# Keys of the second attention: two-part operands and three single-pass products in place of one fp32 product

## The chip, the cores and the metric

The kernel runs on one core of one Trainium2 chip. The metric is the time of one execution on the device in microseconds (us); for the kernel before, the median of three runs is shown. A core has five engines with instruction queues of their own: TensorE (PE in the profile; PEld are its weight loads), VectorE (DVE), ScalarE (ACT), GpSimd (POOL) and SyncE (SP, which only issues DMAs here). They meet through semaphores: an instruction can wait until a counter reaches a value, and can raise one when it is done.

## The reference

The program is two transformer layers on 16 sequences of 128 tokens with 128 features; `ctx_1024` are 16 contexts of 120 rows. Each layer is a cross-attention to the context and a feed-forward part with 8 experts of which 2 are used per token.

```python
x = x + L0_xattn(layernorm(x), ctx, ctx, ...)   # 16 heads of 8 features, a temperature per head from a small MLP
x = x + L0_ffn(layernorm(x), ...)               # top 2 of 8 experts, hidden size 256
x = x + L1_xattn(layernorm(x), ctx, ctx, ...)   # 8 heads of 128 features, windows of 64 positions, dilations 1, 2, 4, 8
x = x + L1_ffn(layernorm(x), ...)               # top 2 of 8 experts, hidden size 64
```

In `L1_xattn` the queries and keys of head h are `x Wq[h]` and `ctx Wk[h]` with biases, and their dot products are the scores. The kernel folds both weights into one matrix per head, so that "keys" of a head are the context times a 128x128 matrix, and the queries are the normalized x itself.

## The kernel before

One program text per engine, written by hand; nothing schedules it, and the order on an engine is the order of the text. A helper, `software_pipeline`, takes stages with lags and writes them out step by step, one sequence after the other (`peel=NB`: no hardware loop). The program has five parts: (a) statistics of the first attention's scores (to about 114 us); (b) the first attention and the routing, with POOL scattering rows to a table in memory sorted by expert (to about 192 us); (c) the first experts, 39 tiles of 128 rows, which PE, ACT and DVE work on while SP loads and stores tiles (to about 257 us); (d) the second attention, sequence by sequence; (e) the second experts, the first of them mixed into the last steps of (d).

The change touches (d). Its operands: `ctxS` holds the 16 contexts, turned and with their rows in an order by dilation, 128 columns each; `qk1` holds the folded matrices of the 8 heads, written by ACT (line 660) at the start of (b); `vo1` the same for values and output. The function `d_keys(p, half)` on PE (lines 1774 to 1783) makes the keys of a pair p of sequences for four heads: four products of a 128x128 matrix with 256 columns of `ctxS`, each into half a PSUM bank, in full fp32. ACT (line 802), and in the first two pairs DVE too (line 1429), adds `uvec` and writes them to `keys`. There are 8 pairs with 2 halves. Four halves (`EARLY_PAIRS = 2`) stand ahead of the pipeline of (d), behind PE's last expert tile; the other twelve are one per step, from the third step on.

A step of (d) on PE: turn the attention weights and the norms (line 1545), keys (1781), output of whole heads (1838), values (1794), scores (1814, 1820), more values (1800, 1804), more output (1843). DVE has in a step: the scores with the window (1436, 1439, 1442), the residual (1461), the two expert rows of a later sequence gathered from memory and added (1413, 1417), norms (1150, 1160, 1178), and the attention weights (1447, 1449, 1453). ACT has the evictions of values (767) and turned weights (794), of norms (710, 697), the exponentials (773, 776) and the keys (802). POOL gathers rows by indirect DMA (983, two per sequence) and does the reciprocal roots (914, 916) and small sums.

Ahead of its gathers POOL has a stretch of its own: the low part `w1_lo` of the second experts' first weights (958), `b2h`, `b2l` and `b2t` (962 to 971) out of their biases. Rounded types (`F32R`, fp32r in the profile) are used in the kernel before already in (e): line 1857 makes a product as high times high, high times low and low times high, and line 1890 multiplies the gates with `b2t`.

Buffers are shared by hand: `shared(name, ...)` lays several tiles over one place, and `area(at, n)` cuts columns from `work`. Here `w1_hi` and `w1_lo` lie over `kT`, the keys of the first attention.

Of the kernel before, what the change touches and what calls it, by code (L numbers as in the profile page):

```python
# [8 lines left out]
F32 = mybir.dt.float32  # L9
F32R = mybir.dt.float32r  # L10
BF16 = mybir.dt.bfloat16
U32 = mybir.dt.uint32
ALU = mybir.AluOpType
# [3 lines left out]
P = 128  # L17


NB, LQ, LK, D = 16, 128, 120, 128  # L20
H0, DK0 = 16, 8
DH0 = 64
NE = 8
HID0 = 256
H1, E1 = 8, 128
# [3 lines left out]
F1 = 64  # L29
# [12 lines left out]
SEQS = 4  # L42
# [167 lines left out]
def build(nc, cols, widths, t, out):  # L210
    with ExitStack() as ctx:
        def sb(name, shape, dt=F32):
            return ctx.enter_context(nc.sbuf_tensor(name, shape, dt))[:]

        def shared(name, shape, parts):

            with nc.sbuf_tensor(name, shape, F32) as a:
                whole = a[:]
            return whole, [sb(*part) for part in parts]

        def sem(name):
            return ctx.enter_context(nc.semaphore(name))

        psum = ctx.enter_context(nc.psum_tensor("psum", [P, 8, 512], F32))
        BANK_KEEP, BANK_TAIL = 7, 6


        first, smalls, late = (sb(name, [P, widths[name]]) for name in ("first", "small", "late"))

        def of_pack(name):  # L230
            for pack, whole in (("first", first), ("small", smalls), ("late", late)):
                if name in cols[pack]:
                    return whole[:, cols[pack][name]]
# [4 lines left out]
        ctxS = sb("ctxS", [P, NB, P])  # L238

        qT, (b2t,) = shared("qT", [P, NB, LQ], [("b2t", [P, 2, 2, SEQS, D], F32R)])  # L240
        kT, (w1_hi, w1_lo, _) = shared("kT", [P, NB, LK], [
            ("w1_hi", [P, NE * F1], F32R), ("w1_lo", [P, NE * F1], F32R), ("kT_rest", [P, NB * LK - 2 * NE * F1], F32)])
        v0 = sb("v0", [LK, NB, D])

        xT, (x_hi,) = shared("xT", [P, NB, LQ], [("x_hi", [P, NB, LQ], F32R)])

# [9 lines left out]
        small = sb("scratch", [P, 8, BH])  # L256
# [6 lines left out]
        routerT, w2T, w3c = of_pack("router0"), of_pack("w2")[0:DH0], of_pack("w3")[0:DH0]  # L263
        w1f = sb("w1f", [P, 3, DH0])
        w1b = of_pack("w1").rearrange("p (c h) -> p c h", c=3)
        qk1 = sb("qk1", [P, H1, D])
        vo1 = sb("vo1", [P, H1, D])
        uvec = sb("uvec", [P, H1])
        router1, rb1, b2rows, b1e = (of_pack(n) for n in ("router1", "rb1", "b2rows", "b1e"))
# [17 lines left out]

        work, (gm, _) = shared("work", [P, 13552], [  # L290
            ("gm", [P, 2, SEQS, LQ], F32R), ("work_rest", [P, 13552 - 2 * SEQS * LQ], F32)])

        def area(at, n):
            return work[:, at:at + n]
# [5 lines left out]
        wcT = area(W_C, 1024).rearrange("p (h o) -> p h o", h=H1)  # L300

        wa, (_, b2h, gT, split, _, c_area, _, rows_r, _) = shared("wa", [P, 8688], [
            ("wa_h1", [P, 2560], F32), ("b2h", [P, D], F32R), ("gT", [P, 2, P], F32R),
            ("split", [P, 2, 2, 2, SEQS * NE], F32R), ("wa_b2l", [P, D], F32), ("c_area", [P, 4096], F32), ("wa_rows", [P, H1_TILES * P], F32),
# [73 lines left out]
        def banks(a, n, parts=P):  # L378
# [4 lines left out]
        rank_ps = keep[:, 512 - SLOTS * NE:512]  # L383
        total_ps = keep[0:1, 192:192 + NE]

        in_c = (area(13184, 12).rearrange("p (z s) -> p z s", z=2), area(13196, 4).rearrange("p (z s) -> p z s", z=2),
                area(13200, 8).rearrange("p (z s) -> p z s", z=2),
                c_area[:, 3840:4096].rearrange("p (z d) -> p z d", z=2), None)

        names = ("bn6", "mv", "rstd", "xn", "xnT")  # L390
# [39 lines left out]
        wt_ps, wt_act = sem("wt_ps"), sem("wt_act")  # L430
# [25 lines left out]
            sem("d_" + n) for n in ("kps", "keys_dve", "keys_act", "s", "sm", "max", "exp", "rs", "a", "tp", "aT", "vwp", "vw", "y", "x"))  # L456
        l1_folded, kept = sem("l1_folded"), sem("kept")
        b_xb, d_xb = sem("b_xb"), sem("d_xb")
        rounded, halved = sem("rounded"), sem("halved")
        e_gt, e_gts, e_h, e_g, e_gm, e_gps, e_hg, e_y, e_acc = (  # L460
            sem("e_" + n) for n in ("gt", "gts", "h", "g", "gm", "gps", "hg", "y", "acc"))
        e_split, e_out = sem("e_split"), [sem("e_out0"), sem("e_out1")]
# [88 lines left out]
        PRODUCTS = 4  # L551
# [38 lines left out]
        def keys_bank(p, half):  # L590
            return 2 * half if p < EARLY_PAIRS else 0
# [235 lines left out]
        def _(pool):  # L827
# [140 lines left out]
            for n in range(4):  # L968
                at, i = divmod(n, 2)
                of, rows = ((b2h[:, :].bitcast(F32), own[:, at, :]), (b2l, by_group[:, at, 0, :]))[i]  # L970
                nc.gpsimd.tensor_tensor(b2t[:, at, i], of.unsqueeze(1).to_broadcast([P, SEQS, D]),
                                        rows.unsqueeze(2).to_broadcast([P, SEQS, D]), ALU.mult).then_inc(halved, 1)

            def gather(b):
                r = b % RING_C
                if b == 0:
                    for s in range(RING_C):
                        pool.wait_ge(st_ct[s], 16 * len(range(s, TILES, RING_C)))
                if b >= RING_C:
                    pool.wait_ge(c_added, b - RING_C + 1)  # L980
                for j in range(2):
                    i = slot_of(j, b)
                    nc.gpsimd.indirect_dma_start(y_rows[:, r, j, :], None, by_expert[:, :],  # L983
                                                 bass.IndirectOffsetOnAxis(rows_at[:, i:i + 1], 0)).then_inc(ld_y[r], 16)
# [558 lines left out]
        def _(pe):  # L1543
            def turn(dst, src, k):
                return nc.tensor.transpose(dst, src, ident[0:k, 0:k])  # L1545
# [97 lines left out]
            for half in range(2):  # L1643
                m = turn(psum[:, 5, half * P:(half + 1) * P], small[:, 2, half * P:(half + 1) * P], P)
# [129 lines left out]
            def d_keys(p, half):  # L1774
                evicted = 2 * p + half if p >= EARLY_PAIRS else 2 * p + half - 1
                if evicted > 0:
                    pe.wait_ge(d_keys_dve, min(evicted, 2 * EARLY_PAIRS))
                    pe.wait_ge(d_keys_act, evicted)
                bank = keys_bank(p, half)
                for i in range(4):  # L1780
                    m = nc.tensor.matmul(psum[:, bank + i // 2, 2 * P * (i % 2):2 * P * (i % 2 + 1)], qk1[:, 4 * half + i, :],  # L1781
                                         ctxS[:, 2 * p:2 * p + 2, :].rearrange("p b s -> p (b s)"), start=True, stop=True)
                m.then_inc(d_kps, 1)

            def d_next_keys(b, z):
                if EARLY_PAIRS <= b // 2 + 1 < NB // 2:
                    d_keys(b // 2 + 1, b % 2)
# [131 lines left out]

            pe.wait_ge(halved, 1)  # L1920
            pe.wait_ge(ld_late, 32)
            for half in range(2 * EARLY_PAIRS):
                d_keys(*divmod(half, 2))
            c_turn = tail_turn("c")
# [46 lines left out]
```

## Time and profile before

| | us |
|---|---|
| median of 3 runs | 415.02 (414.48 to 415.03) |
| the profiled execution's own time | 413.28 |
| its span, first to last instruction | 411.5 |
| PE busy in the span | 353.8 (86%) |
| DVE busy | 303.3 (74%) |
| ACT busy | 271.8 (66%) |
| POOL busy | 196.9 (48%) |
| L1781, the keys, PE busy | 29.8 |

Busy times of engines overlap, so their shares say nothing of what sets the end; that is read from the chain that ended last, which is followed back from the last instruction to what released it at each step, and from the idle times of the engines. The mean duration of a matmul contains its way through the array (380 ns for L1781), and matmuls are pipelined: what one costs in a row of them is the distance between starts. An fp32 product shows as two instructions, a rounded one as one. PEclk is the clock granted to TensorE as a share of 2.4 GHz.

### The profile page before, as it was taken

What the parts mean: (1) busy time and instruction counts of PE and PEld (TensorE: products, weight loads), DVE (VectorE), ACT (ScalarE), POOL (GpSimd) and SP (SyncE); (2) the same over time, 40 slices, a digit from 0 to 9 for tenths busy, and PEclk for the clock granted to TensorE, in tenths of its full rate; (3) what the DMA queues carried; (4) which work ended last, traced back from release to release, by engine and by line L of the source; (5) the groups of instructions that cost most, each with busy time, mean ns of one, the idle gap of its engine ahead of it and who ended that gap; (6) DMA issues with size and microseconds to landing.
All of it is one profiled execution on the core that took longest, in us unless ns stands there. A gap on an engine that the chain in (4) does not pass through costs nothing.

```text
span 411.5 us, 11910 instructions
## 1 busy us (share of the span) xinstructions
PE 353.8 (86%) x4049; PEld 269.5 (65%) x4049; DVE 303.3 (74%) x1127; ACT 271.8 (66%) x813; POOL 196.9 (48%) x295
## 2 busy tenths in 40 slices
PE   2988897682599999973999999888999999968997
PEld 0524362341276767752999998757888888756886
DVE  5399989988428999996764444378898888885852
ACT  2499998986265657542578886457878778672440
POOL 4785878811002215667783000478878783532200
PEclk9988789986589999995799999989999999996999
DMA  7975739700000000112343332111001010000011
GB/s 234 338 212 160 223 100 335 322 1 0 3 2 6 6 5 18 37 34 70 105 116 92 97 92 57 37 33 41 27 23 28 17 28 2 2 2 2 4 49 51
DMA packets 36202, 30.97 MB, mean 75 GB/s; under 512 B 3504, under 2 KB 33584, under 8 KB 35504
## 3 DMA queue, kind: packets, MB, share of 16 engines
q1 hardware_dynamic: 33520, 24.98, 19.2%
q0 software_dynamic: 2048, 4.20, 3.5%
q10 hardware_dynamic: 576, 1.05, 0.7%
q8 instruction: 33, 0.54, 0.6%
q14 instruction: 25, 0.20, 0.2%
HBM read 14.94 MB, written 15.14 MB: 73 GB/s over the span
## 4 chain that ended last, share of the span: by engine, by line
PE 56%; DVE 19%; ACT 9%; issue 8%; POOL 4%; DMA 4%; POOLq 0%; DVEq 0%; SPq 0%; ACTq 0%
PE psum L1753 9%; ACT wa L649 6%; PE psum L1705 5%; PE psum L1545 4%; PE psum L1781 4%; PE psum L1764 4%; DVE scored L1089 3%; DVE scored L1076 3%; PE psum L1585 3%; PE psum L1894 3%; PE psum L1804 2%; PE psum L1688 2%; PE psum L1857 2%; DVE work L1131 2%; PE psum L1820 2%
## 5 line engine op out<-in xcount | busy, mean ns | idle before, releaser
L649 ACT ACTIVATE wa<-psum,scored 128x120 f32<-128x120 f32 x256 | 69.5, 436 | 3.8 <-DVE scored L1076 3.8
L983 POOL DMA_INDIRECT c_area<-by_expert,rows_at x32 | 31.4, 980 | 51.3 <-DMA by_expert<-c_area 39.7
L1089 DVE BATCH_NORM_STATS2 scored<-wa 128x6 f32<-128x240 f32 x128 | 43.1, 398 | 1.6 <-issue 0.8
L1076 DVE TENSOR_REDUCE scored<-psum 128x8 f32<-128x960 f32 x32 | 36.5, 1142 | 9.9 <-PE psum L1585 9.9
L682 ACT ACTIVATE work<-psum 120x1024 f32<-120x1024 f32 x32 | 31.0, 1021 | 18.8 <-PE psum L1693 18.8
L1753 PE MATMUL psum<-c_area,work 128*128 128x128 f32 x312 | 43.3, 284 | 0.0
L1585 PE MATMUL psum<-wa,qT 64*128 64x480 f32 x128 | 41.0, 725 | 2.3 <-ACT wa L649 2.3
L1753 PEld LDWEIGHTS psum<-c_area,work 128*128 128x128 f32 x312 | 39.7, 200 | 0.1
L910 POOL TENSOR_TENSOR rstd<-rstd,eps 128x2 f32<-128x2 f32 x16 | 12.5, 784 | 55.0 <-DVE rstd L1165 55.0
L866 POOL TENSOR_TENSOR wa<-kT,first 128x960 f32<-128x960 f32 x16 | 28.6, 1791 | 16.6 <-PE psum L1585 16.6
L942 POOL DMA_INDIRECT by_expert<-scored,rows_at x32 | 32.2, 1006 | 8.9 <-issue 8.3
L1335 DVE TENSOR_TENSOR c_area<-psum,c_area 128x256 f32<-128x256 f32 x39 | 16.5, 424 | 26.4 <-ACT c_area L748 22.9
L1781 PE MATMUL psum<-ctxS,qk 128*128 128x256 f32 x128 | 29.8, 380 | 0.0
L773 ACT ACTIVATE work<-work,d 128x128 f32<-128x128 f32 (+1 forms) x64 | 23.1, 370 | 5.8 <-DVE d L1439 5.8
L743 ACT COPY work<-upT 128x512 f32 x39 | 24.2, 621 | 2.4 <-issue 2.4
L767 ACT COPY work<-psum 128x1024 f32<-128x1024 f32 x16 | 16.2, 1011 | 14.0 <-PE psum L1804 13.9
L1781 PEld LDWEIGHTS psum<-ctxS,qk 128*128 128x128 f32 x128 | 23.7, 193 | 2.6
L1764 PE MATMUL psum<-dnT,c_area 128*128 x156 | 24.4, 280 | 0.6 <-DVE c_area L1335 0.6
L802 ACT ACTIVATE work<-psum,uvec 128x256 f32<-128x256 f32 x56 | 22.0, 471 | 2.7 <-PE psum L1781 2.7
L782 ACT ACTIVATE wa<-psum,late 128x512 f32<-128x512 f32 x16 | 10.8, 685 | 19.2 <-DVE c_area L1476 10.8
L1131 DVE RECIPROCAL work<-psum 128x128 f32<-128x128 f32 x16 | 15.3, 954 | 10.0 <-PE psum L1705 9.5
L748 ACT ACTIVATE c_area<-psum 128x256 f32<-128x256 f32 x39 | 14.9, 383 | 11.1 <-PE psum L1753 11.1
(264 smaller groups left out, 945.0 us busy)
## 6 DMA issues: line engine op xcount, KB each, us to landing
by_expert<-work SPq DMA_DIRECT2D x12, 768.0 KB, 7.6
c_area<-by_expert SPq DMA_DIRECT2D x39, 64.0 KB, 1.8
by_expert<-c_area SPq DMA_DIRECT2D x39, 64.0 KB, 1.6
upT<-in_up_dram SPq DMA_DIRECT2D x1, 2048.0 KB, 13.7
work<-in_heads_dram SPq DMA_DIRECT2D x1, 1536.0 KB, 8.9
late<-in_late_dram SPq DMA_DIRECT2D x1, 1098.0 KB, 10.3
x<-in_x_dram ACTq DMA_DIRECT2D x4, 256.0 KB, 5.6
ctxS<-in_ctx_classes_dram SPq DMA_DIRECT2D x1, 1024.0 KB, 10.0
```

Of the source, the lines that this page charges most:

```text
L649: e = nc.scalar.activation(prob[:, z, head, :], psum[:, score_bank(b, half) + h // 4, (h % 4) * LK:(h % 4 + 1) * LK], ACT.Exp, bias=rowneg ...
L682: nc.scalar.activation(probT[:, z, half * HALF0:(half + 1) * HALF0, :].rearrange("p h q -> p (h q)"), psum[0:LK, 2 * half:2 * half + 2, :] ...
L743: nc.scalar.copy(ct_w[:, n % 2, :], upT[:, bass.ds(e * UP_TILES, UP_TILES), :].rearrange("p t c -> p (t c)")).then_inc(ct_we, 1)
L866: nc.gpsimd.tensor_tensor(kexp[:, z], kT[:, b, :].unsqueeze(1).to_broadcast([P, HALF0, LK]), halfscale.unsqueeze(2).to_broadcast([P, HALF0 ...
L942: nc.gpsimd.indirect_dma_start(by_expert[:, :], bass.IndirectOffsetOnAxis(rows_at[:, i:i + 1], 0), xrow[:, BATCH * r + i % BATCH, :], None ...
L983: nc.gpsimd.indirect_dma_start(y_rows[:, r, j, :], None, by_expert[:, :], bass.IndirectOffsetOnAxis(rows_at[:, i:i + 1], 0)).then_inc(ld_y ...
L1076: nc.vector.tensor_reduce(rowneg[:, b * H0:(b + 1) * H0].rearrange("p (a c h) -> p a c h", a=2, c=2)[:, :, half], banks(score_bank(b, half ...
L1089: s = nc.vector.bn_stats(bnout[:, bass.ds(b * HALF0 + h // 2, 1), :].rearrange("p a s -> p (a s)"), prob[:, z, h:h + 2, :].rearrange("p h ...
L1585: m = nc.tensor.matmul(psum[:, score_bank(b, half) + g, 0:4 * LK], qT[rows, b, :], kexp[rows, z, 4 * half:4 * half + 4].rearrange("p i k - ...
L1753: m = nc.tensor.matmul(psum[:, n % 2, j * P:(j + 1) * P], ct_w[:, n % 2, j * P:(j + 1) * P], ct_xT[:, n % 2, :], start=True, stop=True)
L1764: m = nc.tensor.matmul(psum[:, 4, 0:D], ct_h[:, n % 2, j * P:(j + 1) * P], w, start=(j == 0), stop=(j == DN_TILES - 1))
L1781: m = nc.tensor.matmul(psum[:, bank + i // 2, 2 * P * (i % 2):2 * P * (i % 2 + 1)], qk1[:, 4 * half + i, :], ctxS[:, 2 * p:2 * p + 2, :].r ...
```

## The change

Every key product becomes three products of rounded operands (fp32r) that are summed in PSUM: high part of the matrix times high part of the context, high times low, and low times high. The high part is the operand rounded by a cast, the low part is the operand less its high part, rounded. POOL makes the four arrays once, between the biases `b2t` and the first gather: `qk_lo` (first used for the rounded copy), `ctx_hi`, then `qk_lo` itself, `qk_hi` over `qk1`'s own place, and `ctx_lo`. PE waits for the fifth of these ahead of its first keys.

Places: `w1_lo` moves over the first attention's weights in `first`; `qk_lo` lies over `kT`, `ctx_hi` over `v0`, `ctx_lo` over columns 11264 to 13312 of `work`, and the small tiles of the c norms move from column 13184 to 13448.

```diff
-        kT, (w1_hi, w1_lo, _) = shared("kT", [P, NB, LK], [
+        kT, (w1_hi, qk_lo, _) = shared("kT", [P, NB, LK], [
...
-        qk1 = sb("qk1", [P, H1, D])
+        qk1, (qk_hi,) = shared("qk1", [P, H1, D], [("qk_hi", [P, H1, D], F32R)])
...
+            pool.wait_ge(wt_act, PRODUCTS)
+            nc.gpsimd.tensor_copy(qk_lo[:, :, :], qk1[:, :, :]).then_inc(split_keys, 1)
+            nc.gpsimd.tensor_copy(ctx_hi[:, :, :], ctxS[:, :, :]).then_inc(split_keys, 1)
+            pool.wait_ge(split_keys, 1)
+            nc.gpsimd.tensor_tensor(qk_lo[:, :, :], qk1[:, :, :], qk_lo[:, :, :].bitcast(F32), ALU.subtract).then_inc(split_keys, 1)
+            pool.wait_ge(split_keys, 3)
+            nc.gpsimd.tensor_copy(qk_hi[:, :, :], qk1[:, :, :]).then_inc(split_keys, 1)
+            nc.gpsimd.tensor_tensor(ctx_lo[:, :, :], ctxS[:, :, :], ctx_hi[:, :, :].bitcast(F32), ALU.subtract
+                                    ).then_inc(split_keys, 1)
...
                 for i in range(4):
-                    m = nc.tensor.matmul(psum[:, bank + i // 2, 2 * P * (i % 2):2 * P * (i % 2 + 1)], qk1[:, 4 * half + i, :],
-                                         ctxS[:, 2 * p:2 * p + 2, :].rearrange("p b s -> p (b s)"), start=True, stop=True)
+                    for j, (left, right) in enumerate(((qk_hi, ctx_hi), (qk_hi, ctx_lo), (qk_lo, ctx_hi))):
+                        m = nc.tensor.matmul(psum[:, bank + i // 2, 2 * P * (i % 2):2 * P * (i % 2 + 1)], left[:, 4 * half + i, :],
+                                             right[:, 2 * p:2 * p + 2, :].rearrange("p b s -> p (b s)"), start=(j == 0), stop=(j == 2))
                 m.then_inc(d_kps, 1)
...
             pe.wait_ge(halved, 1)
             pe.wait_ge(ld_late, 32)
+            pe.wait_ge(split_keys, 5)
             for half in range(2 * EARLY_PAIRS):
                 d_keys(*divmod(half, 2))
```

On PE, a step of (d) with a half of the keys (row L1781), before (names: `psum<-` and the two operands, then the output's size and how many follow each other; an fp32 product is one row entry here):

```order
L1545 MATMUL psum<-first,c_area 128x128
L1781 MATMUL psum<-ctxS,qk 128x256 x4
L1838 MATMUL psum<-work 128x128 x2
L1794 MATMUL psum<-vo,ctxS 128x256
L1814 MATMUL psum<-work,xT 128x256
L1820 MATMUL psum<-work,xT 32x128 x8
```

The same place now; lines have moved by 13 to 16, and the three rows of L1797 are the last of the four heads' triples:

```order
L1797 MATMUL psum<-ctx_hi,qk_hi 128x256
L1797 MATMUL psum<-ctx_lo,qk_hi 128x256
L1797 MATMUL psum<-ctx_hi,qk_lo 128x256
L1854 MATMUL psum<-work 128x128 x2
L1810 MATMUL psum<-vo,ctxS 128x256
L1830 MATMUL psum<-work,xT 128x256
L1836 MATMUL psum<-work,xT 32x128 x8
```

Four products have become twelve; nothing else of the step has moved on PE. On POOL, the end of its own stretch and the first gather, before (in brackets the semaphores waited for):

```order
L971 TENSOR_TENSOR b2t<-b2h,own 128x512 [waits halved,b_qexp]
L971 TENSOR_TENSOR b2t<-wa,first 128x512
L971 TENSOR_TENSOR b2t<-b2h,own 128x512
L971 TENSOR_TENSOR b2t<-wa,first 128x512
L983 DMA c_area<-by_expert,rows_at 128x128 [waits st_ct2,st_ct3,st_ct1,st_ct0]
```

And now:

```order
L976 TENSOR_TENSOR b2t<-wa,first 128x512
L980 CAST qk_lo<-qk 128x1024 [waits wt_act]
L981 CAST ctx_hi<-ctxS 128x2048
L983 TENSOR_TENSOR qk_lo<-qk,qk_lo 128x1024 [waits split_keys]
L985 CAST qk_hi<-qk 128x1024 [waits split_keys]
L986 TENSOR_TENSOR ctx_lo<-ctxS,ctx_hi 128x2048
L998 DMA c_area<-by_expert,rows_at 128x128 [waits st_ct2,st_ct3,st_ct1,st_ct0]
```

Five instructions have come in between the biases and the gather. DVE, ACT and SP have the same instructions in the same order as before.

## Rows read from the trace of the kernel before

**Rows 1.** The page's costliest groups; the key products (busy us, mean ns, idle before).

```profile
L1781 PE MATMUL psum<-ctxS,qk 128*128 128x256 f32 x128 | 29.8, 380 | 0.0
```

**Rows 2.** Windows: length, busy us of PE, PEld, DVE, ACT, POOL, PEclk, DMA share, GB/s.

```profile
266.00:268.00 2.00, 0.22 (x1) 0.14 (x1) 1.56 (x6) 0.00 (x0) 1.29 (x3) 1.00 0.00 0
268.00:272.00 4.00, 3.45 (x29) 1.64 (x32) 2.04 (x9) 1.36 (x2) 3.20 (x5) 0.62 0.13 33
...
280.00:346.00 66.00, 64.77 (x1104) 56.68 (x1092) 57.08 (x248) 53.45 (x175) 51.07 (x95) 1.00 0.09 24
...
366.00:372.00 6.00, 2.47 (x28) 1.83 (x28) 5.57 (x24) 5.53 (x17) 1.44 (x4) 0.94 0.00 0
372.00:378.00 6.00, 5.44 (x28) 4.19 (x29) 2.61 (x10) 0.69 (x1) 1.43 (x4) 0.50 0.01 3
```

**Rows 3.** The chain that ended last (start us, us, engine, tile, line), second attention.

```profile
261.31 3.73 DMA c_area<-by_expert,rows_at
...
283.00 0.77 PE psum L1545 x5
283.77 1.73 PE psum L1781 x8
...
340.70 1.73 PE psum L1781 x8
...
346.67 0.68 DVE work L1436
```

**Rows 4.** PE in order of time, second experts.

```profile
385.01 0.39 PE L1857 MATMUL psum<-x_hi,w_lo 128*128 128x512 f32 x1
385.25 0.40 PE L1890 MATMUL psum<-b2t,gT 128*128 128x256 f32 x2
385.48 1.95 PE L1894 MATMUL psum<-late,c_area 128*128 128x128 f32 x16
387.18 0.48 PE L1890 MATMUL psum<-b2t,gT 128*128 128x256 f32 x2
387.50 1.95 PE L1894 MATMUL psum<-late,c_area 128*128 128x128 f32 x16
```

**Rows 5.** One step in order of time, all engines (start us, us, engine, instruction).

```profile
301.26 1.01 ACT L767 COPY work<-psum 128x1024 f32<-128x1024 f32 x1 [1.17 <-PE psum L1804]
...
305.02 0.28 DVE L1447 TENSOR_REDUCE d<-work 128x4 f32<-128x128 f32 x1 [0.48 <-ACT work L776]
...
305.57 0.99 DVE L1453 TENSOR_TENSOR work<-work,d 128x256 f32<-128x256 f32 x3
...
307.91 0.33 PE L1545 MATMUL psum<-first,work 128*128 128x128 f32 x1
```

**Rows 6.** DVE in order of time, first steps of the second attention.

```profile
282.86 0.68 DVE L1436 TENSOR_TENSOR work<-psum,late 128x512 f32<-128x512 f32 x1
...
289.04 0.68 DVE L1436 TENSOR_TENSOR work<-psum,late 128x512 f32<-128x512 f32 x1
...
293.54 1.09 DVE L1453 TENSOR_TENSOR work<-work,d 128x256 f32<-128x256 f32 x3
...
294.81 0.68 DVE L1436 TENSOR_TENSOR work<-psum,late 128x512 f32<-128x512 f32 x1
...
300.51 0.68 DVE L1436 TENSOR_TENSOR work<-psum,late 128x512 f32<-128x512 f32 x1
```

**Rows 7.** PE in order of time, first steps of the second attention.

```profile
295.22 0.66 PE L1545 MATMUL psum<-first,work 128*128 128x128 f32 x4
```

**Rows 8.** Groups of POOL by form (busy us, mean ns).

```profile
L927 POOL TENSOR_TENSOR x_lo<-xnT,x_hi 128x128 fp32r<-128x128 f32 x16 | 7.6, 472 | 1.3
...
L925 POOL CAST x_hi<-xnT 128x128 fp32r<-128x128 f32 x16 | 4.5, 283 | 1.8 <-ACT xnT L710 1.8
```

**Rows 9.** POOL in order of time, ahead of the gathers.

```profile
219.16 1.04 POOL L971 TENSOR_TENSOR b2t<-wa,first 128x512 fp32r<-128x512 f32 x1
259.91 1.09 POOL L983 DMA_INDIRECT c_area<-by_expert,rows_at  x1 [39.70 <-DMA by_expert<-c_area]
```

More of the change, by code:

```diff
@@ L225, in build @@
         BANK_KEEP, BANK_TAIL = 7, 6
-        first, smalls, late = (sb(name, [P, widths[name]]) for name in ("first", "small", "late"))
+        first, (w1_lo, _) = shared("first", [P, widths["first"]], [
+            ("w1_lo", [P, NE * F1], F32R), ("first_rest", [P, widths["first"] - NE * F1], F32)])
+        smalls, late = (sb(name, [P, widths[name]]) for name in ("small", "late"))
         def of_pack(name):
@@ L240, in build @@
         qT, (b2t,) = shared("qT", [P, NB, LQ], [("b2t", [P, 2, 2, SEQS, D], F32R)])
-        kT, (w1_hi, w1_lo, _) = shared("kT", [P, NB, LK], [
-            ("w1_hi", [P, NE * F1], F32R), ("w1_lo", [P, NE * F1], F32R), ("kT_rest", [P, NB * LK - 2 * NE * F1], F32)])
-        v0 = sb("v0", [LK, NB, D])
+        kT, (w1_hi, qk_lo, _) = shared("kT", [P, NB, LK], [
+            ("w1_hi", [P, NE * F1], F32R), ("qk_lo", [P, H1, D], F32R), ("kT_rest", [P, NB * LK - NE * F1 - H1 * D], F32)])
+        v0_rows, (ctx_hi,) = shared("v0", [P, NB, D], [("ctx_hi", [P, NB, P], F32R)])
+        v0 = v0_rows[0:LK]
         xT, (x_hi,) = shared("xT", [P, NB, LQ], [("x_hi", [P, NB, LQ], F32R)])
@@ L286, in build @@
         xnT = sb("xnT", [P, 2, LQ])
-        work, (gm, _) = shared("work", [P, 13552], [
-            ("gm", [P, 2, SEQS, LQ], F32R), ("work_rest", [P, 13552 - 2 * SEQS * LQ], F32)])
+        W_LOW = 11264
+        work, (gm, _, ctx_lo, _) = shared("work", [P, 13552], [
+            ("gm", [P, 2, SEQS, LQ], F32R), ("work_mid", [P, W_LOW - 2 * SEQS * LQ], F32), ("ctx_lo", [P, NB, P], F32R),
+            ("work_rest", [P, 13552 - W_LOW - NB * P], F32)])
         def area(at, n):
@@ L384, in build @@
         total_ps = keep[0:1, 192:192 + NE]
-        in_c = (area(13184, 12).rearrange("p (z s) -> p z s", z=2), area(13196, 4).rearrange("p (z s) -> p z s", z=2),
-                area(13200, 8).rearrange("p (z s) -> p z s", z=2),
+        in_c = (area(13448, 12).rearrange("p (z s) -> p z s", z=2), area(13460, 4).rearrange("p (z s) -> p z s", z=2),
+                area(13464, 8).rearrange("p (z s) -> p z s", z=2),
                 c_area[:, 3840:4096].rearrange("p (z d) -> p z d", z=2), None)
@@ L458, in build @@
         b_xb, d_xb = sem("b_xb"), sem("d_xb")
-        rounded, halved = sem("rounded"), sem("halved")
+        rounded, halved, split_keys = sem("rounded"), sem("halved"), sem("split_keys")
         e_gt, e_gts, e_h, e_g, e_gm, e_gps, e_hg, e_y, e_acc = (
```

## The prediction

> **What bounds the kernel now.** I read the page's costliest groups first, then the windows with the clock, the chain that ended last, one step of the second attention engine by engine, and last the rows that hold the new form of instruction. The group of L1781 is what the change edits: 128 instructions for 64 fp32 products, so two instructions a product, 29.8 us of TensorE (PE) busy time [rows 1]. Where they stand decides what they are worth. From 280 to 346 us PE is busy 64.77 of 66 us at the full clock, 2.4 GHz, and every other engine has room [rows 2]; the chain runs there through PE alone, and one half of the keys, 1.73 us, comes round in each step from 283.77 to 340.70 us: ten halves at nine intervals, (340.70 − 283.77)/9 = 6.33 us a step [rows 3]. In that stretch the step is PE's own sum, and what PE loses in work the step loses.
>
> Outside it the halves are not on the path. The first four stand before 264 us, while the chain goes through the gather's DMA (261.31, 3.73 us); PE is busy only 0.22 us from 266 to 268 [rows 2, 3]. The half before 283 us is followed by a wait of PE for VectorE (DVE), since the chain comes from POOL and DVE there and enters PE only at 283.00 [rows 3]. The twelfth half of the loop stands after 346.67 us, where the chain has passed to DVE's scores and the expert choice [rows 3]. So 10 halves of 16 count.
>
> **What a half costs before and after.** Before: 4 products, 8 instructions, 1.73 us, or 0.216 an instruction with two passes over 256 columns. After: 4 × 3 = 12 instructions of one pass over the same 256 columns, rounded operands (fp32r), each with a weight load of 128 columns as now. The trace holds that form: the two 128x256 fp32r products of L1890 start at 385.25 and the next line at 385.48, 0.115 each; the 512-column one ahead takes 385.25 − 385.01 = 0.24, about the double [rows 4]. So a half becomes 12 × 0.115 = 1.38 us, and a step loses 0.35. Ends: at the tempo of a pass of the old instructions, 0.216/2 = 0.108, a half is 1.30 and the step loses 0.43; in the other L1890 pair, whose two products take 387.50 − 387.18 = 0.32 [rows 4], one costs 0.16, a half 1.92, and the step grows by 0.19. I take 0.115, since the products of a half stand in a row without a wait, as at 385.25, where the pair at 387.18 follows a wait and other work. Break-even is 1.73/12 = 0.144.
>
> Beside the row of 0.115, the Trainium skill ("FP8 and Floating Point Precision", TensorE Precision Notes) has an fp32 product as four passes, high and low parts each with each; by that three passes of four would be 1.30 us, and the sum 10 × 0.43. The row of L1890 lies nearer and decides.
>
> **Who is late next.** In a step of the stretch VectorE waits 0.48 us for ScalarE's (ACT's) exponentials (305.02), and ACT waits 1.17 us for PE (301.26): both follow PE and come earlier with it. The last of DVE's products that PE turns ends at 305.57 + 0.99 = 306.56, PE reaches the turn at 307.91 [rows 5]: 1.35 us to spare, of which 0.35 go. Without that wait DVE fills 6.33 − 0.48 = 5.85 us of a step, so at 5.98 it still fits. ACT's evictions of the keys (after the exponentials) keep their place. One place gives something back: early in the stretch DVE is behind. Its product of 293.54 ends at 294.63, and PE turns it at 295.22 [rows 6, 7]. Two shortened halves ahead would bring PE there at 295.22 − 0.70 = 294.52, so PE waits some 0.15 to 0.2 us, once, as DVE's next round (294.81 to 300.51, 5.70 us [rows 6]) is shorter than PE's 5.98. I subtract 0.2.
>
> **What is added.** GpSimd (POOL) gets five instructions ahead of the gathers: casts of 1024, 2048 and 1024 columns, differences of 1024 and 2048. No row has these sizes. From below: nothing less than zero. From above, by the 128-column rows times 8 and 16, with the fixed part of each counted as often: casts 0.283 × 32 = 9.1, differences 0.472 × 24 = 11.3, together 20.4 us [rows 8]. They start behind POOL's last product, 219.16 + 1.04 = 220.2, and POOL does nothing until the gather at 259.91, a wait of 39.70 us for the expert stage's stores [rows 9]. Ending at 240.6 at the latest, they are done before PE's first keys at about 257, whose new wait stands behind the last expert tile: cost 0. Queued behind that wait are the keys, values and turns, nothing else; behind the casts on POOL the gathers and the normalizations, which wait anyway. Without the cover a microsecond past 259.9 would cost a microsecond. The casts' own wait is for copies of the first attention's stage, long past. The new places of the buffers (the low part of the expert weights, the small tiles at 13448) move no instruction; on ACT, DVE and SP the order stays as it was.
>
> **The sum.** 10 × 0.35 − 0.2 = 3.3 us. The profiled execution takes 413.28 us, span 411.5 and 1.8 around it; 413.28 − 3.3 = 409.98. The median of the runs shown is 415.02, 1.74 above that execution; added again, 411.7 us. The likeliest case's own range is 410.4 to 413.4: 0.43 or about 0.2 saved a step (411.0 or 413.2), and some 0.6 below or 0.2 above for the spread of the runs shown.
>
> **Rivals.** *Clock.* The granted clock is 0.62 from 268 to 272 us and 0.50 (1.2 GHz) from 372 to 378, each time after PE had been idle for much of the time (busy 0.22 of 2 us and 2.47 of 6 just ahead); the later stretch has 5.44 us of PE work [rows 2]. The change makes PE idle 1.4 us earlier ahead of 268 (four halves, 0.35 each) and moves the later stretch against the clock's falls. If the second fall is missed, half of 5.44, 2.7 us, is won: 409.0. If one falls as long on work now at full clock, 2.7 are lost: 414.4. For it: both falls stand at PE's idle places, which move. Against: the idle places remain, with the same length at the later one. The first is worth less: 3.45 us at 0.62 would be 2.1 at the full clock, 1.3 us [rows 2]. Chance 7% each way.
>
> *DVE takes over.* If DVE's rounds cannot follow, with its waits for ACT and POOL, and stay near the 6.18 us of one early round (scores at 282.86 and 289.04), a step loses only 0.15: 1.5 us, 413.5. For it: that round, and how little of a step DVE has free. Against: its rounds of 5.77 and 5.70 us right after [rows 6], and ACT's part, which PE releases. Chance 14%.
>
> *Weight loads stand outside: slower.* In a half 12 loads follow each other instead of 8, behind shorter products. If a load isn't drawn ahead, the pair at 387.18 [rows 4] gives the price: 0.16 a product, 1.92 a half, 0.19 × 10 = 1.9 us more, 416.9. It decides from 0.144 a product on. Against: the pair at 385.25 has two loads and takes 0.115 each. Chance 8%.
>
> On this the Trainium skill ("TensorE: Matmul & The Clock Gate", Part 3, The mechanism) says that a weight load overlaps a running product only where the row groups differ, and here all 128 rows are used. By that rule each of the loads would stand beside its product and the kernel would be slower, as in this rival. The trace speaks against it, with 0.115 for a load and a product of 256 columns.
>
> That the rounded operands would not bring single passes I leave out: 0.115 for 256 columns excludes it.
>
> **How the numbers follow.** Forecast 64%, clock 14%, DVE 14%, loads 8%. What a measurement of this kernel can tell from no change is 0.2%, 0.83 us, so faster means under 414.2. Faster: 62 of the 64, 7 of the clock, 12 of DVE's 14: 81%. Slower, over 415.85: the 8 of the loads and 1 of the others: 9%. The same: 10%. The range reaches on the low side to the won clock and on the high side past DVE's case and the lost clock: 409.0 to 414.6.
>
> **What would show it.** In the profile of the changed kernel: 12 of PE's instructions in a half, where there are 8, and 1.38 us for it on the chain, steps of 5.98 us between 280 and 343 us, DVE's wait for ACT at about 0.13; POOL's splits between 220 and 241 and the first gather still at about 260 behind the store's DMA and no wait of PE's for the splits. Wrong it would be if a half takes 1.7 us or more, if steps stay at 6.2 or above with PE waiting for DVE, if the gather moves, or if PE works at 1.2 GHz in another stretch than 268 to 272 and 370 to 376.

## The result, and the profile after

The changed kernel takes 411.5 us (median, 410.25 to 413.72) and the kernel before 415.02 (413.4 to 417.01) on the same chip: ratio 0.9923, 95% interval 0.9899 to 0.9946, so 2.2 to 4.2 us faster. The forecast was 411.7. On another chip, with two altered kernels beside it, the same changed kernel took 410.51 against 415.78 (0.9883, 0.984 to 0.9927).

The profiled execution takes 411.19 us, its span is 409.4 (before 411.5). The answers to [rows 1] are the key products of the page before, now three groups by operands (columns: count, then shortest, median and longest in ns, first and last start):

```profile
L1797 PE MATMUL psum<-ctx_hi,qk_hi x64: 279/280/365, 258.6 to 345.8; 128*128 128x256 f32 x64
L1797 PE MATMUL psum<-ctx_lo,qk_hi x64: 278/281/290, 258.8 to 345.9; 128*128 128x256 f32 x64
L1797 PE MATMUL psum<-ctx_hi,qk_lo x64: 277/281/285, 258.9 to 346.1; 128*128 128x256 f32 x64
```

192 instructions where there were 128, but what one costs in a row of them is the distance of starts. PE in order of time, a half of the changed kernel and what follows it:

```profile
302.45 0.36 PE L1797 MATMUL psum<-ctx_hi,qk_hi 128*128 128x256 f32 x1
302.65 0.28 PE L1797 MATMUL psum<-ctx_lo,qk_hi 128*128 128x256 f32 x1
302.76 0.28 PE L1797 MATMUL psum<-ctx_hi,qk_lo 128*128 128x256 f32 x1
302.88 0.28 PE L1797 MATMUL psum<-ctx_hi,qk_hi 128*128 128x256 f32 x1
...
303.82 0.28 PE L1797 MATMUL psum<-ctx_hi,qk_lo 128*128 128x256 f32 x1
303.95 0.61 PE L1854 MATMUL psum<-work 128*128 128x128 f32 x4
```

From 302.65 to 303.82 ten products pass, 0.117 to 0.118 each. The windows that answer to [rows 2], shifted by the gain (length, busy us of PE, PEld, DVE, ACT and POOL, PEclk, DMA share, GB/s):

```profile
268.00:272.00 4.00, 2.78 (x21) 1.42 (x21) 2.29 (x9) 1.36 (x2) 3.22 (x6) 0.80 0.12 33
...
280.00:343.00 63.00, 61.69 (x1128) 55.56 (x1132) 56.40 (x241) 53.77 (x177) 50.87 (x95) 1.00 0.10 26
363.00:369.00 6.00, 3.06 (x37) 2.42 (x35) 5.54 (x26) 5.65 (x16) 1.44 (x4) 1.00 0.00 0
369.00:375.00 6.00, 4.81 (x30) 3.65 (x29) 2.80 (x9) 1.06 (x3) 1.43 (x4) 0.53 0.00 0
```

PE is still busy almost throughout from 280 to 343 us (61.69 of 63), at 2.4 GHz; the stretch at about 1.2 GHz behind PE's idle place is there as before. The chain that ended last, against [rows 3]:

```profile
262.98 2.94 DMA c_area<-by_expert,rows_at
...
283.47 0.95 POOL c_area L998
...
287.33 0.95 POOL c_area L998
...
290.32 0.82 DVE d L1454 x3
...
291.80 0.68 PE psum L1854 x4
...
296.66 1.42 PE psum L1797 x12
...
302.69 1.42 PE psum L1797 x12
```

A half is 1.42 us where it was 1.73. But the chain runs through POOL's gathers and DVE until 291.80 us; before, PE held it from 283.00 on. Two of the halves are no longer on it.

From the starts of the halves in PE's order of time, the span divides so (us; k0 to k11 are the loop's halves, and "the ramp" is from here on the stretch from the first keys to k1):

| stretch | before | after | difference |
|---|---|---|---|
| start to the first keys | 256.95 | 258.55 | +1.60 |
| first keys to k1 (the ramp) | 26.66 | 25.41 | −1.25 |
| k1 to k3 | 12.50 | 12.45 | −0.05 |
| k3 to k11, eight steps | 50.77 | 48.27 | −2.50 |
| k11 to the end | 64.62 | 64.72 | +0.10 |

The steps go from 6.34 or 6.35 to 6.03 or 6.04: 8 × 0.31 = 2.5. In the first row the change has only POOL's splits, and its +1.60 is not shown to come from them: with the splits and fp32 keys (split_only, below) the first keys start at 257.37, and three more executions of the changed kernel, two of them with a few instructions more, have 257.30, 257.53 and 258.88. The +0.10 of the last row lies within what it varies by in the runs below (64.4 to 64.7). The ramp is looked into below.

### The profile page after: what moved, and what is told of

Same layout as the page of the kernel before. It is cut to its first block, busy times and chain, and to the rows that moved or that the text cites. A ratio compares the mean times of both kernels' runs of the same rounds, so it can differ in the third digit from the quotient of the medians.

```text
span 409.4 us, 12043 instructions
## 1 busy us (share of the span) xinstructions
PE 350.1 (86%) x4113; PEld 269.2 (66%) x4113; DVE 303.5 (74%) x1127; ACT 272.1 (66%) x813; POOL 206.9 (51%) x300
## 4 chain that ended last, share of the span: by engine, by line
PE 52%; DVE 21%; issue 9%; ACT 7%; POOL 5%; DMA 3%; POOLq 0%; DVEq 0%; SPq 0%; ACTq 0%
PE psum L1768 8%; PE psum L1720 5%; PE psum L1560 4%; PE psum L1779 4%; DVE scored L1104 4%; ACT wa L654 4%; DVE scored L1091 3%; PE psum L1600 3%; PE psum L1910 3%; PE psum L1797 2%; PE psum L1703 2%; PE psum L1873 2%; POOL c_area L998 2%; PE psum L1820 2%; DVE work L1146 2%
## 5 line engine op out<-in xcount | busy, mean ns | idle before, releaser
L787 ACT ACTIVATE wa<-psum,late 128x512 f32<-128x512 f32 x16 | 10.8, 685 | 19.1 <-DVE c_area L1491 9.3
L772 ACT COPY work<-psum 128x1024 f32<-128x1024 f32 x16 | 16.2, 1012 | 10.9 <-PE psum L1820 10.8
L1560 PE MATMUL psum<-first,c_area 128*128 128x128 f32 x55 | 16.2, 295 | 6.7 <-DMA c_area<-by_expert 3.4
L1779 PEld LDWEIGHTS psum<-dnT,c_area 128*128 128x128 f32 x156 | 21.0, 196 | 0.8 <-issue 0.8
```

Source lines behind the costliest of these rows:

```text
L1779: m = nc.tensor.matmul(psum[:, 4, 0:D], ct_h[:, n % 2, j * P:(j + 1) * P], w, start=(j == 0), stop=(j == DN_TILES - 1))
```

## The experiments

All timed runs stand beside the kernel before on the same chip; ratios are to it, with 95% intervals. The first four kernels edit one line of the changed kernel, the list of products in a half:

```diff
-                    for j, (left, right) in enumerate(((qk_hi, ctx_hi), (qk_hi, ctx_lo), (qk_lo, ctx_hi))):
+                whole = ((qk_hi.bitcast(F32), ctxS),)
+                parts = ((qk_hi, ctx_hi), (qk_hi, ctx_lo), (qk_lo, ctx_hi))
+                taken = parts if 7 <= 2 * p + half < 15 else whole   # step_halves
+                taken = whole if 7 <= 2 * p + half < 15 else parts   # ramp_halves
+                taken = whole                                        # split_only
+                taken = parts[0:1]                                   # hi_only
```

**step_halves**, the three products only in the eight halves k3 to k10:

> The three rounded products only in eight halves of the keys, the ones of the fourth to the eleventh step with keys (on the chain from 296 to 339 us in the profile of the changed kernel); the other eight halves are one fp32 product of the rounded matrix again (the matrix's low part is left out there). Theory A (only the halves in PE's own steps count, and these are eight, not ten): the whole gain of the steps, 8 x 0.31 = 2.5 us, so 412.5 against 415.0, and 1 us above the changed kernel only by whatever the ramp gave. Theory B (ten halves count): 2 x 0.31 less than the changed kernel's steps give. Theory C (a third of the gain came ahead of the steps, from the earlier end of the first four halves): the time from the first turn to the first keys of the loop as in the kernel before.

Measured 411.69 us, ratio 0.9935 (0.991 to 0.9961): 2.7 us faster, 1.6 to 3.7. Its chain shows both kinds of halves:

```profile
289.77 1.73 PE psum L1800 x8
296.11 1.42 PE psum L1800 x12
```

Steps of 6.03 and 6.04 from k3 on. The eight halves alone bring their 2.5 us.

**ramp_halves**, the other eight halves:

> The complement: the three rounded products in the first four halves, the first three of the loop and its last, and one fp32 product of the rounded matrix in the eight halves between (the matrix's low part is left out there). Theory A: steps of 6.33 us as before, no gain within what can be told: 415.0, ratio 1.000. Theory B: the halves of the second and third step count, 0.6 us: 414.4. Theory C: up to 1.2 us from the ramp: 413.8.

Measured 413.13 us, ratio 0.9975 (0.9942 to 1.0009): unclear, between 2.4 us faster and 0.4 slower. Steps of 6.35. Its profiled execution has a short ramp, 24.71 us instead of 26.66, but its first keys start at 260.07, 3.1 us later than before.

**split_only**, POOL's splits and PE's wait with one fp32 product:

> The splits on POOL and PE's wait for them stay, all sixteen halves are one fp32 product of the rounded matrix again (its low part is left out). If the splits cost nothing behind the wait for the stores: 415.0, ratio 1.000, splits of 10.8 us on POOL between 220 and 233 us, the gather still behind the DMA. If they take something from the expert tiles (DVE or PE beside POOL's long instructions): tiles above 1.45 us in that stretch, the time up by as much, at most 1 us.

Measured 414.09 us, ratio 0.9991 (0.9967 to 1.0015): no cost that shows (1.4 us less to 0.6 more). The steps are 6.35, the ramp 26.62. The splits are not on the path.

**hi_only**, one of the three products (the two with low parts are left out):

> Only the first of the three products, high part by high part: the other two are left out. A half has 4 instructions of 0.118 us, 0.47 instead of 1.42. If PE alone sets the step, the step falls from 6.03 to 5.08 us, 8 steps give 7.6 us more and the kernel takes 404. If DVE is next at about 5.85 us of own work and waits, the step stops near 5.7 to 5.85, 8 steps give 1.5 to 2.6 us, and it takes 409 to 410, with PE waiting for DVE in every step.

Measured 408.98 us, ratio 0.9857 (0.9822 to 0.9893). Steps of 5.61 to 5.77, with one of 6.06, instead of the 5.09 that PE's work alone would allow (6.03 − 8 × 0.118). The window of the stretch, and one row of PE in order of time:

```profile
280.00:340.00 60.00, 52.79 (x996) 45.13 (x995) 54.37 (x234) 52.64 (x174) 49.59 (x91) 1.00 0.11 28
```

```profile
304.99 0.68 PE L1857 MATMUL psum<-work 128*128 128x128 f32 x4 [0.38 <-DVE x L1476]
```

PE is busy 52.79 of 60 us, DVE 54.37, PE waits for DVE in the step, and the chain runs there through DVE: DVE is the next bound, at about 5.65 us a step, 0.4 below the changed kernel's. It is the fastest kernel measured, but another computation: rounded operands alone.

**four_products**, the changed kernel with low × low added, 16 instructions a half:

```diff
-                    for j, (left, right) in enumerate(((qk_hi, ctx_hi), (qk_hi, ctx_lo), (qk_lo, ctx_hi))):
+                taken = (*parts, (qk_lo, ctx_lo))
```

> The changed kernel with the fourth product, low x low, added: 16 matmuls a half instead of 12, output the reference's. Theory of a sum by the number of products in the eight steps in which TensorE works without a wait: a half 16 x 0.118 = 1.89 us instead of 1.42, so a step of 6.03 + 0.47 = 6.50, and 8 x 0.47 = 3.8 us more than the changed kernel, some 415.3 (ratio to before 1.000 to 1.003; 8 x 0.15 = 1.2 us more than before in the steps, up to 1 us less in the ramp). If all twelve halves counted it would be 5.6 more, 417.1 (1.005). If something else than the number of products set the step (a wait for VectorE or ScalarE), the step would stay near 6.1 and the time near 412.

```profile
292.02 1.88 PE psum L1800 x16
```

Measured 416.4 us, ratio 1.0007 (0.9967 to 1.0046). A half is 1.88 = 16 × 0.118 and a step 6.50 or 6.51, 0.47 more than the changed kernel, as worked out. With all four products nothing is left of the gain: it lies in the product left out.

**The ramp: where TensorE's program is loaded.** The traces so far had ramps of 24.7 to 26.7 us, and the first gather's landing (from its issue on POOL to DVE's first use) went with them. The next kernels repeat a wait that is long satisfied, which puts instructions without work into PE's program (48 repeats add 24 instructions to its trace, 320 add 160) and so moves the places where it is loaded.

```diff
-            pe.wait_ge(l1_folded, 5)
+            for _ in range(49): pe.wait_ge(l1_folded, 5)     # before_pad, after_pad
+            for _ in range(321): pe.wait_ge(l1_folded, 5)    # before_pad160
```

> The kernel before with 48 repeats of a wait that is long satisfied, at one place early in TensorE's program where TensorE waits anyway (about 24 instructions without work); nothing else is changed. The traces so far show that the ramp between the first keys and the loop is shorter where the four early halves have rounded keys, and that the first gather lands 4.36, 3.92 and 4.40 us after its issue there (after, ramp_halves, hi_only) against 5.16, 5.13 and 4.86 (before, split_only, step_halves). In the slow ones one packet of the queue 'instruction' (0.02 MB, TensorE's program) falls 2.5 us behind the gather's issue. Theory 'fetch': that packet holds back one DMA engine's share of the gather; 24 instructions at about 0.108 us bring it 2.6 us earlier, to the issue or ahead of it, and the gather lands after about 3.9 us instead of 5.16: the stretch from the first keys to the loop's fourth half goes from 39.2 to about 38, and the kernel to about 413.8 (ratio 0.997). Steps of the loop stay 6.35. Rival 'keys': TensorE's keys themselves (less weight data, another pace) let the gather land sooner; then nothing changes here: landing 5.1, ratio 1.000 +- 0.001. Third: the stretch is noise of the clock, then the landing moves without the stretch.

Measured 415.24 us, ratio 1.0016 (0.9983 to 1.0049); the packet stayed at 2.6 us behind the issue, so this run can't tell the theories apart.

> The changed kernel with the same 48 repeats of a satisfied wait, nothing else. In it the packet of TensorE's program falls 2.0 us behind the gather's issue. Theory 'fetch': 24 instructions at 0.06 us bring it 1.4 us earlier, to 0.5 us behind, as in ramp_halves, where the gather landed after 3.92: landing from 4.36 to about 3.9, time 0.4 us less than the changed kernel (about 411.1 against before at 415.0, ratio 0.9905 to 0.992). Rival 'keys': landing 4.4, ratio 0.9923 as measured for the changed kernel.

Measured 409.77 us, ratio 0.9875 (0.9831 to 0.9919). The packet went further than meant, to 3.2 us ahead of the issue, onto the last store ahead of the gathers. The DMA of that run from 257.5 to 259 us (queue: packets, MB, share of the 16 engines' time; then an issue with its KB and us to landing):

```profile
q1 hardware_dynamic: 240, 0.11, 25.8%
q8 instruction: 1, 0.02, 4.4%
...
by_expert<-c_area SPq DMA_DIRECT2D x1, 64.0 KB, 2.4
```

The store lands after 2.41 us instead of 1.53, the gather after 4.00 instead of 4.36.

> The kernel before with 320 repeats of the satisfied wait, that is 160 instructions without work instead of 24. With 24 the packet of TensorE's program stayed where it was, 2.6 us behind the gather's issue (TensorE's next instructions stand behind a wait there, so 24 more of them do not bring the fetch forward), and the landing stayed at 5.0 us. 160 instructions are more than TensorE has between the last wait of the second part and the first wait of the turn (about 120 by the program), so that packet has to fall ahead of the first keys' waits, at 259 us or earlier, and the next one some 8 us later. Theory 'fetch': the gather lands 3.9 to 4.0 us behind its issue instead of 5.0 to 5.2, and the stretch from the first keys to the loop's fourth half goes from 39.2 to about 38.2; time 0.2 to 0.3% under before if the 160 instructions cost nothing at TensorE's wait of 5.8 us. Rival 'keys' (the rounded keys themselves let the gather land sooner): landing 5.0 to 5.2, no change of the stretch. four_products speaks against the rival already (rounded keys, packet 2.8 us behind the issue, landing 5.1).

Measured 422.27 us, ratio 1.0156 (1.0106 to 1.0206): slower. The profiled execution, 425.94 us and the longest of the six, shows PE idle for 16.57 us at the place of the 160 instructions, where it had waited 5.82 before:

```profile
113.06 1.08 PE L1631 MATMUL psum<-scored,w1f 128*64 128x256 f32 x2 [16.57 <-issue]
```

The stretch asked for is far behind that. DMA from 262 to 263.5 us before, and at the same distance from the gather's issue (277 to 278.5) in before_pad160:

```profile
q0 software_dynamic: 45, 0.06, 17.0%
q8 instruction: 1, 0.02, 5.1%
```

```profile
q0 software_dynamic: 32, 0.07, 17.6%
```

The packet is gone from there, and with fp32 keys unchanged the gather lands 4.03 us behind its issue (before 5.16):

```profile
274.49 1.09 POOL L983 DMA_INDIRECT c_area<-by_expert,rows_at  x1 [40.15 <-DMA by_expert<-c_area]
...
278.52 0.35 DVE L1413 SCALAR_TENSOR_TENSOR x<-c_area,ew_t,x 128x128 f32<-128x128 f32 x1 [0.92 <-DMA c_area<-by_expert,rows_at]
```

So the gather lands sooner without rounded keys, where the packet is out of its way; with rounded keys and the packet behind the issue (four_products) it lands as late as before. Its ramp, 24.74 us, is 1.9 shorter than before's: 1.13 of that is the landing, and the granted clock over the ramp was 1.00 against 0.94, which is the rest, as shown below. Last, the changed kernel with and without the 24 instructions on one chip:

> The changed kernel, unaltered, on the same chip as the next one, so that the two can be compared directly: 411.5 against before at 415.0, ratio 0.992.

> The changed kernel with 48 repeats of the satisfied wait, beside the changed kernel on the same chip. In its first run the packet of TensorE's program fell 3.2 us ahead of the gather's issue and the gather landed after 4.00 instead of 4.36 us; the time was 409.8. If only that landing is behind it, it is 0.3 to 0.5 us faster than the changed kernel here; if the first run's 1.7 us hold, something else moved with the packet; if it was chance, the two agree within 0.2%.

Measured 410.51 (ratio 0.9883, 0.984 to 0.9927) and 411.31 (0.989, 0.9835 to 0.9944): no difference that shows. The 1.7 us between the first runs of the two are not confirmed, and the expected 0.3 to 0.5 can't be told. The same program also had its packet at another place in its second profiled execution. All profiled executions, in the order of their landing (us; the packet of queue q8 against the gather's issue, from windows of a quarter microsecond; "scores" is what PE's first scores behind the gather take, from their start to the start of the values that follow, with the clock granted meanwhile):

| kernel | packet | landing | scores (PEclk) | ramp |
|---|---|---|---|---|
| before | +2.6 | 5.16 | 1.94 (0.57) | 26.66 |
| split_only | +2.7 | 5.13 | 1.93 (0.57) | 26.62 |
| four_products | +2.8 | 5.12 | 1.82 (0.60) | 26.51 |
| before_pad | +2.6 | 5.01 | 2.07 (0.53) | 26.65 |
| step_halves | +2.5 | 4.86 | 1.73 (0.64) | 26.19 |
| after_again | +2.4 | 4.75 | 1.98 (0.56) | 26.30 |
| hi_only | +1.5 | 4.40 | 2.16 (0.50) | 26.26 |
| after | +2.2 | 4.36 | 1.50 (0.78) | 25.41 |
| before_pad160 | −5.5 | 4.03 | 1.20 (1.00) | 24.74 |
| after_pad | −3.2 (on the store) | 4.00 | 1.72 (0.64) | 26.21 |
| ramp_halves | +0.6 | 3.92 | 1.20 (1.00) | 24.71 |
| after_pad_again | +0.8 | 3.84 | 1.21 (0.99) | 24.66 |

Landing follows the packet: 4.75 to 5.16 where it falls 2.4 us or more behind the issue, 3.84 to 4.03 where it falls 0.8 behind or less, or ahead. The ramp is longer or shorter by two terms, the landing and the scores. The other pieces are alike in all twelve: 2.65 to 2.76 us from the landing to the first turn, 0.87 to 1.02 from there to the scores, 12.92 to 13.05 from the end of the scores to k1 (only after_pad has its gather 0.9 later, by the late store). How long the scores take follows the granted clock: 1.20 us at 2.4 GHz, 2.16 at 1.2 GHz, and between these where the clock is at the lower level for only a part of them. They stand on the chain that ended last, before and in the changed kernel:

```profile
268.66 1.00 PE psum L1814 x2
269.66 1.06 PE psum L1820 x16
```

```profile
269.54 0.70 PE psum L1830 x2
270.24 0.89 PE psum L1836 x16
```

So of the 1.25 us that the ramp of the changed kernel's first profile is shorter, 0.80 are the landing and 0.44 the clock. Neither comes with the changed kernel each time: its second profiled execution (after_again) has 4.75 and 1.98. What decides where the stretch at 1.2 GHz begins is not shown.

## Why the prediction was right

*The time* was right, 411.7 against 411.5, and the sign. That it fell within 0.2 us is partly luck: where the sum has 3.3 us, the steps give 2.5 and the two halves ahead of them 0.05. The spans of the profiled executions lie about that far apart, 2.1 to 3.1 us (before, split_only and before_pad 411.5 to 411.9; the changed kernel and after_pad, twice each, 408.8 to 409.4). The medians of the timed runs differ by 3.5 us, with an interval of 2.2 to 4.2 (on the other chip 3.0 to 6.7); what lies above 2.5 is not explained.

*A half* was given as 12 × 0.115 = 1.38 and is 1.42, 0.118 a product; the step loses 0.31, not 0.35. The pair of L1890 in [rows 4] was the right row and read 0.003 short. (The low end of its own range, for 0.43 a step, comes to 410.9, not 411.0.) Against the tempo of the old instructions, 0.108 a pass, each short product costs 0.010 more. The Trainium skill (FP8 and Floating Point Precision, TensorE Precision Notes) gives an fp32 product as four passes; three of four would have been 1.30. The trace is near that count, with 0.47 for four rounded products against 0.43 for one fp32 product, but a pass does not cost the same in both forms. The rival with the weight loads outside is refuted: a product comes every 0.118 us, under the break-even of 0.144, and PE and PEld are busy 61.69 and 55.56 of the same 63 us, so loads lie beside products with all 128 rows in use. By the sentence of the Trainium skill that the prediction took (TensorE: Matmul & The Clock Gate, Part 3, The mechanism) they would not, though the same section also lets a load into a background weight buffer be drawn ahead. Here the measurement decides.

*Ten halves on the path* was the step that failed. Eight shorten their steps, k3 to k10: 2.50 us by the table, and step_halves alone shows 6.03 a step. (On the changed kernel's own chain they are seven: it leaves PE ahead of k10, at 339 us, for ACT and DVE. What k10 gives at the end is not told apart.) The halves k1 and k2 were to give 0.70, less 0.2 for one wait of PE for DVE at the turn of 295.22 [rows 7]. They gave 0.05. At that turn, 295.60 now, PE does not wait. It waits a step earlier, ahead of the output of whole heads, for DVE's residual:

```profile
288.78 0.35 DVE L1178 TENSOR_SCALAR xn<-x,mv,rstd 128x128 f32<-128x128 f32 x1 [0.47 <-POOL rstd L916]
290.81 0.28 DVE L1461 TENSOR_TENSOR x<-psum,x 128x128 f32<-128x128 f32 x1
291.50 0.61 PE L1838 MATMUL psum<-work 128*128 128x128 f32 x4
```

```profile
289.34 0.35 DVE L1193 TENSOR_SCALAR xn<-x,mv,rstd 128x128 f32<-128x128 f32 x1 [0.71 <-POOL rstd L921]
291.35 0.28 PE L1797 MATMUL psum<-ctx_hi,qk_lo 128*128 128x256 f32 x1
291.37 0.28 DVE L1476 TENSOR_TENSOR x<-psum,x 128x128 f32<-128x128 f32 x1
291.80 0.68 PE L1854 MATMUL psum<-work 128*128 128x128 f32 x4 [0.17 <-DVE x L1476]
```

Before (first fence; rows of both engines, not all), the residual ends 0.41 us ahead of PE's start at 291.50; now it ends at 291.65 and PE has to wait. The 0.17 of the row has the size of the forecast wait by chance. By the starts it costs 0.32: 0.45 us lie between the last key product and L1854, where 0.13 are enough at 303.82. What sets DVE there is the chain of POOL's gathers up to 288 us, which PE's shorter halves do not move: the prediction took the point where PE enters the chain, 283.00 [rows 3], as fixed, while a shorter half moves that point back behind the other engines.

*The first four halves at nothing* is not refuted: ramp_halves is unclear at −1.0 us (−2.4 to +0.4). In the profiles nothing is won ahead of the loop: k1 starts at 283.5 to 284.0 us in the four profiles of the changed kernel and after_pad, and at 283.6, 284.0 and 283.9 in before, split_only and before_pad (284.8 in ramp_halves). The 1.25 us of the first profile's ramp are offset by its later first keys, and after_again, the same program, has a ramp of 26.30. A change of PE's program moves the packet that holds the gather up; whether the timed runs gain by that on the average, these runs do not settle.

*Who is late next* came as forecast. One step of the changed kernel, against [rows 5]:

```profile
301.34 1.01 ACT L772 COPY work<-psum 128x1024 f32<-128x1024 f32 x1 [0.86 <-PE psum L1820]
...
305.09 0.29 DVE L1462 TENSOR_REDUCE d<-work 128x4 f32<-128x128 f32 x1
...
305.65 0.99 DVE L1468 TENSOR_TENSOR work<-work,d 128x256 f32<-128x256 f32 x3
...
307.67 0.66 PE L1560 MATMUL psum<-first,work 128*128 128x128 f32 x4
```

DVE's wait of 0.48 is gone, and its last product ends at 306.64, 1.03 us before PE turns it (1.00 expected). That DVE's rounds stay near 6.18 is refuted by the steps of 6.03; hi_only shows where they do end, at about 5.65.

*The splits* were bounded at 20.4 us and cost 10.8, hidden as forecast ([rows 8, 9]). POOL in order of time:

```profile
221.61 1.04 POOL L980 CAST qk_lo<-qk 128x1024 fp32r<-128x1024 f32 x1
222.59 1.89 POOL L981 CAST ctx_hi<-ctxS 128x2048 fp32r<-128x2048 f32 x1
224.44 2.36 POOL L983 TENSOR_TENSOR qk_lo<-qk,qk_lo 128x1024 fp32r<-128x1024 f32 x1
226.87 1.04 POOL L985 CAST qk_hi<-qk 128x1024 fp32r<-128x1024 f32 x1
227.86 4.54 POOL L986 TENSOR_TENSOR ctx_lo<-ctxS,ctx_hi 128x2048 fp32r<-128x2048 f32 x1
261.59 1.09 POOL L998 DMA_INDIRECT c_area<-by_expert,rows_at  x1 [29.18 <-DMA by_expert<-c_area]
```

They end at 232.4, and POOL still waits 29.18 us for the store. A cast of 8 times the columns took 1.04, not 8 × 0.283 = 2.26.

*The clock* rival did not come in the later stretch: PE at about 1.2 GHz from 369 to 375 us (0.53), 4.81 us of work there, before 5.44 at 0.50 [rows 2]. Of the first fall, priced at up to 1.3 us, 0.44 came in the first profile, in the scores of the ramp, and none in after_again.

## What to carry to other kernels

Three rounded products of 256 columns took 0.35 us, one fp32 product 0.43 and four rounded ones 0.47: the gain is the part left out, less what each short product costs more. Count the rounds that gain from the point where the engine holds the chain *after* the change, not before: at the seam, where another engine was only just ahead, two halves gave 0.05 us instead of 0.62. And before a small gain outside the bound stretch is put down to a change, look at a second profile of the same kernel: two executions of one program differed by 0.9 us in this ramp, and two of another by 1.6, by when one store and one gather landed and by the clock under one group of products.

## What the runs showed of the hardware that was not expected

An engine's program comes by DMA too, in packets of 16 KB on a queue of its own (q8, 33 or 34 packets, 0.54 or 0.56 MB in a run), and one of them among a gather's packets goes with a landing 0.7 to 1.3 us later, among a store's 0.9 (1.53 to 2.41 us). Where it falls changes with the program's length and from one execution to the next.

160 instructions without work gave PE an idle time of 16.57 us, ended by issue, where it had waited 5.82 us before; 24 cost nothing there (5.85). By an estimate from the first number one takes 0.10 us, so 24 take 2.5 and fit into the wait.

The same two groups of products took 1.20 us at 2.4 GHz and 2.16 at 1.2 GHz, and between executions of one program the fall of the clock stood at another place among them (1.50 and 1.98 us; 1.72 and 1.21).
